# Turning h by transposing transfers in every tile of a state-space scan with a quantized gated FFN

## The reference

```
xc = conv(in_proj(ctx));  u = silu(xc + b)
dt = softplus(dt_proj(x_proj(u)[:16]) + b);  B, C = x_proj(u)[16:32], x_proj(u)[32:48]
state = state * exp(dt * A) + (dt * u) * B      # 16 states, over 512 positions
y = (sum over the states of state * C + D * u) * silu(layernorm(x))
x = x + tanh(g_x) * y

def bitlinear(x, w):                  # activations and weights fake-quantized
    xq = round(clip(rms(x) * s)) / s          # s = 127 / max|rms(x)|
    wq = round(clip(w / mean|w|, -1, 1)) * mean|w|
    return xq @ wq.T
n = layernorm(x)
h = silu(bitlinear(n, w_gate)) * bitlinear(n, w_up)      # 2048 wide
x = x + tanh(g_ffn) * bitlinear(h, w_down)
```

## Time and profile before

| | |
|---|---|
| median of 3 runs | 612.37 us (612.18 to 612.91) |
| the profiled execution | 611.89 us, of it 609.9 us span |
| busy: PE, PEld | 516.7 us (85%), 359.8 us (59%) |
| busy: DVE, ACT, POOL | 556.6 us (91%), 507.7 us (83%), 521.0 us (85%) |
| L889 POOL, b products | 117, 2364 ns each |
| L515 and L509 PE, transposes | 1024 and 528 |
| L615 PE, transposes of h | 176, 24.0 us in all |
| transfers of b, c | 1024.0 KB and 512.0 KB, median 6.7 and 6.5 us to landing |

### The profile page before, as it was taken

The page is one execution under the profiler, slowest core; times in us unless marked ns, Lnnn a source line. Parts: engine busy times, 40 slices in busy tenths (PEclk is TensorE's granted clock), DMA queues, the critical chain, the costliest instruction groups (busy, mean ns, idle before and its releaser), DMA issues. The chain is left out here.

```text
span 609.9 us, 9603 instructions
## 1 busy us (share of the span) xinstructions
PE 516.7 (85%) x3190; PEld 359.8 (59%) x3190; DVE 556.6 (91%) x766; ACT 507.7 (83%) x776; POOL 521.0 (85%) x298
## 2 busy tenths in 40 slices
PE   6999676768675888989879898989789999998997
PEld 2443265747564676767656767675667575764443
DVE  1899989999999899999899999998999999988774
ACT  3879788986999789899978898998798989777773
POOL 1558799999999899999999899999998999973340
PEclk9999859778799999999999999999999999999999
DMA  8992951530661010115521111145411110000323
GB/s 273 403 412 108 325 197 34 192 136 1 240 243 53 0 53 2 35 34 208 203 93 35 34 37 36 35 157 223 121 35 35 36 36 18 1 18 21 84 53 86
DMA packets 38866, 66.32 MB, mean 109 GB/s; under 512 B 12177, under 2 KB 20369, under 8 KB 36002
## 3 DMA queue, kind: packets, MB, share of 16 engines
q1 hardware_dynamic: 38818, 65.72, 30.9%
HBM read 55.49 MB, written 8.13 MB: 104 GB/s over the span
## 5 line engine op out<-in xcount | busy, mean ns | idle before, releaser
L889 POOL TENSOR_TENSOR area_s<-area_s,b_bc 128x1024 f32<-128x1024 f32 x117 | 275.2, 2364 | 14.1 <-DVE u_all L1510 9.9
L515 PE MATMUL pY<-ident,area_s 128*128 128x128 f32 x532 | 87.9, 291 | 54.5 <-DVE area_s L1518 54.5
L584 PE MATMUL pG<-wq_gu,area_f 128*128 128x512 fp8e4 x448 | 108.0, 380 | 4.2 <-ACT area_f L1106 2.9
L1510 DVE TENSOR_TENSOR_SCAN area_s<-pA,area_s 128x512 f32<-128x512 f32 x88 | 105.1, 1205 | 5.1 <-ACT pA L1169 5.1
L515 PEld LDWEIGHTS pY<-ident,area_s 128*128 128x128 f32 x532 | 62.2, 146 | 75.4 <-DVE area_s L1518 67.9
L1169 ACT ACTIVATE pA<-dt_all,a_neg 128x512 f32<-128x512 f32 x145 | 97.7, 682 | 10.7 <-DVE area_s L1510 5.9
L881 POOL TENSOR_TENSOR u_all<-u_all 128x1024 f32<-128x1024 f32 x44 | 103.9, 2361 | 0.2 <-DMA u_all<-bc_rows 0.2
L1518 DVE TENSOR_TENSOR area_s<-area_s,pC 128x512 f32<-128x512 f32 x132 | 87.0, 661 | 0.9 <-DVE area_s L1510 0.8
L509 PE MATMUL pC<-ident,xdT 128*128 128x128 f32 x528 | 84.2, 288 | 3.2 <-DVE area_s L1518 2.0
L584 PEld LDWEIGHTS pG<-wq_gu,area_f 128*128 128x128 bf16 x448 | 41.6, 98 | 48.9 <-ACT area_f L1106 5.2
L509 PEld LDWEIGHTS pC<-ident,xdT 128*128 128x128 f32 x528 | 65.4, 146 | 8.1 <-DVE area_s L1518 6.6
(11 more groups left out here) (218 smaller groups left out, 1123.0 us busy)
## 6 DMA issues: line engine op xcount, KB each, us to landing
b_bc<-bc_rows SPq DMA_DIRECT2D x14, 1024.0 KB, 6.7
area_s<-x SPq DMA_DIRECT2D x32, 256.0 KB, 2.9
u_all<-bc_rows SPq DMA_DIRECT2D x14, 512.0 KB, 6.5
b_bc<-w_gate SPq DMA_DIRECT2D x1, 4096.0 KB, 14.0
dt_all<-x SPq DMA_DIRECT2D x1, 4096.0 KB, 24.3
area_f<-w_up SPq DMA_DIRECT2D x1, 4096.0 KB, 33.6
area_f<-w_down SPq DMA_DIRECT2D x1, 4096.0 KB, 14.9
out<-area_f SPq DMA_DIRECT2D x16, 256.0 KB, 2.1
```

Source lines behind the costliest of these rows:

```text
L515: mm = pe.matmul(pY[:, k * P:(k + 1) * P], src[:, k * P:(k + 1) * P], ident[:, :], is_transpose=True, start=(first and k == 0), stop=(last ...
L584: mm = pe.matmul(bank, xqT[t % 2][:, k, :], wq_gu[:, k, m, c * GW:(c + 1) * GW], start=(k == 0), stop=(k == NT - 1))
L889: gp.tensor_tensor(db[c % NDB], du[s % 2].rearrange("p (a l) -> p a l", a=1).to_broadcast([P, CH, L]), b_bc[:, CH * c:CH * c + CH, :], ALU ...
L1510: dve.tensor_tensor_scan(h, at, dbu, 0.0, ALU.mult, ALU.add).then_inc(S["s_scan"], 1)
```

## The change

For tiles 0 to 10 TensorE's 16 transposes of h and ScalarE's four copies out of pG are gone. After scaling a half of h, ScalarE copies it, less MAGIC, as bf16 integers into the first half of the same place (`h_int`, function `whole_h`, semaphore f_ha), at n = 6 and 7. SP then issues a transposing transfer from there to `hqT` (`turn_whole`), the second half's when the first has landed. Since h of the next tile is written to the same place, `gate_silu` of chunk 0 waits for the first transfer and that of chunk 2 for the second. In the loading steps `turn_whole` stands behind three pieces of b and one of c; the fourth piece of b and the other three of c stand behind it. `down` of every tile waits for f_hqD. The tiles from 11 on are turned as before.

```diff
 
+        h_int = [carve(area_f, 1024 * i, F // 4, BF16) for i in range(2)]
         hb = [u_all[:, 2 + 2 * i:4 + 2 * i, :].rearrange("p n l -> p (n l)").bitcast(BF16) for i in range(2)]
...
 
-            def load_c(b):
+            def load_c(b, pairs=range(NP)):
                 for j, pair in enumerate(pooled(NT * b)):
+                    if j not in pairs:
+                        continue
                     if b and j < len(pooled(NT * b - 1)):
...
             load_u(3)
+            def turn_whole(t):
+
+                past(sp, S["f_dn"], t - 1)
+                for i in range(2):
+                    past(sp, S["f_hqD"], 32 * t + 16 * i)
+                    sp.wait_ge(S["f_ha"], 2 * t + i + 1)
+                    sp.dma_start_transpose(hqT[t % 2][:, i * FK // 2:(i + 1) * FK // 2, :], h_int[i]).then_inc(S["f_hqD"], 16)
+
             for s in range(NT, UNITS):
...
                 if s % NT == 0:
-                    load_b(s // NT)
-                    load_c(s // NT)
+                    load_b(s // NT, (0, 1, 2))
+                    load_c(s // NT, (0,))
+                if s >= 6:
+                    turn_whole(s - 6)
+                if s % NT == 0:
+                    load_b(s // NT, (3,))
+                    load_c(s // NT, (1, 2, 3))
                     load_c_alone(s // NT)
...
                 for i in range(2):
-                    past(sp, S["f_hqD"], 32 * (t - DMA_FROM) + 16 * i)
+                    past(sp, S["f_hqD"], 32 * t + 16 * i)
                     sp.wait_ge(S["f_hb"], 2 * (t - DMA_FROM) + i + 1)
...
 
+            turn_whole(DMA_FROM - 1)
             store(UNITS - 7)
...
                     pe.wait_ge(S["f_xqT"], t + 1)
-                    past(pe, S["f_hqT"], HR * t)
                 else:
...
 
-            def hq_transpose(t, r, banks):
-                pe.wait_ge(S["f_hm"], 2 * t + r // 2 + 1)
-                past(pe, S["f_hqT"], HR * t + r - 1)
-                for k in range(4):
-                    mm = pe.transpose(banks[r % 2][:, k * P:(k + 1) * P], h_of(t)[:, (4 * r + k) * P:(4 * r + k + 1) * P], ident[:, :])
-                mm.then_inc(S["f_hqp"], 1)
-
             def down(t, part, z_done):
                 if part == 0:
-                    if t < DMA_FROM:
-                        pe.wait_ge(S["f_hqT"], HR * t + HR)
-                    else:
-                        pe.wait_ge(S["f_hqD"], 32 * (t - DMA_FROM) + 16)
+                    pe.wait_ge(S["f_hqD"], 32 * t + 16)
                     past(pe, S["f_o"], t)
...
                 for k in range(part * DK, min(part * DK + DK, FK)):
-                    if k == FK // 2 and t >= DMA_FROM:
-                        pe.wait_ge(S["f_hqD"], 32 * (t - DMA_FROM) + 32)
+                    if k == FK // 2:
+                        pe.wait_ge(S["f_hqD"], 32 * t + 32)
                     mm = pe.matmul(pT[:, :], hqT[t % 2][:, k, :], wq_dn[:, k, :], start=(k == 0), stop=(k == FK - 1))
...
                 y_sum_pooled(s, 0)
-                if t2 >= 0:
-                    if t1 % NT:
-                        pe.wait_ge(S["f_xqT"], t1 + 1)
-                    hq_transpose(t2, 0, pG)
-                    hq_transpose(t2, 1, pG)
                 fill(s, 4, DPARTS)
-                if t2 >= 0:
-                    hq_transpose(t2, 2, pG)
-                    hq_transpose(t2, 3, pG)
                 y_sum(s, 6)
...
                     past(pe, S["f_h"], FC * t1)
-                    past(pe, S["f_hqT"], HR * t1 - 1)
                     xq_transpose(t1, pG[0])
...
                 act.wait_ge(S["f_gate"], FC * t + c + 1)
-                if t <= UNITS - NT:
-                    past(act, S["f_hqp"], HR * (t - (1 if t < UNITS - NT else 2)) + HR)
-                else:
+                if t < UNITS - NT and t and c % 2 == 0:
+                    act.wait_ge(S["f_hqD"], 32 * (t - 1) + (32 if c else 16))
+                elif t > UNITS - NT:
                     act.wait_ge(S["f_hb"], 2 * (t - 2 - DMA_FROM) + 2)
...
                 if t == UNITS - 1:
-                    act.wait_ge(S["f_hqD"], 32 * (t - 2 - DMA_FROM) + 32)
+                    act.wait_ge(S["f_hqD"], 32 * (t - 2) + 32)
                     junk = hb[t % 2]
...
 
-            def copy_hqT(t, r, banks):
-                act.wait_ge(S["f_hqp"], HR * t + r + 1)
-                past(act, S["f_dn"], t - 1)
-                act.activation(hqT[t % 2][:, 4 * r:4 * r + 4, :], banks[r % 2].rearrange("p (k t) -> p k t", t=P),
-                               ACT.Copy, bias=-MAGIC).then_inc(S["f_hqT"], 1)
+            def whole_h(t, i):
+
+                act.wait_ge(S["f_hm"], 2 * t + i + 1)
+                act.activation(h_int[i], h_main[:, i * F // 2:(i + 1) * F // 2], ACT.Copy, bias=-MAGIC).then_inc(S["f_ha"], 1)
 
...
                         copy_xqT(t1, pG[0][:, :])
+                    if n in (6, 7) and t2 >= 0:
+                        whole_h(t2, n - 6)
                     if n in (5, 6) and t2 >= 0:
...
                         x_variance(t1 + 1)
-                    if n in (7, 8) and t2 >= 0:
-                        copy_hqT(t2, 2 * n - 14, pG)
-                        copy_hqT(t2, 2 * n - 13, pG)
                     if s == PE_FROM - 1 and n in (2, 4, 6, 8):
...
```

More of the change, by code:

```diff
@@ L654, in down_quarter @@
             def down_quarter(t, r):
-                pe.wait_ge(S["f_hqT"], HR * DMA_FROM + r + 1)
+                pe.wait_ge(S["f_hqT"], r + 1)
                 for k in range(4 * r, 4 * r + 4):
@@ L803, in _ @@
                         end_transpose(1)
-                    pe.wait_ge(S["f_hqD"], 32 * (t - 1 - DMA_FROM) + (32 if k else 16))
+                    pe.wait_ge(S["f_hqD"], 32 * (t - 1) + (32 if k else 16))
                 mm = pe.matmul(down_bank(t - 1), hqT[(t - 1) % 2][:, k, :], wq_dn[:, k, :], start=(k == 0), stop=(k == FK - 1))
@@ L960, in h_whole @@
             def h_whole(t):
-                past(gp, S["f_hqD"], 32 * (t - DMA_FROM - 1))
+                past(gp, S["f_hqD"], 32 * (t - 1))
                 whole = [h_of(t)[:, i * F // 2:(i + 1) * F // 2] for i in range(2)]
@@ L967, in h_whole @@
                     if i == 0:
-                        gp.wait_ge(S["f_hm"], 2 * DMA_FROM + t - DMA_FROM + 1)
+                        gp.wait_ge(S["f_hm"], DMA_FROM + t + 1)
                     else:
@@ L1332, in _ @@
             for r in range(HR):
-                act.wait_ge(S["f_hqp"], HR * DMA_FROM + r + 1)
+                act.wait_ge(S["f_hqp"], r + 1)
                 act.activation(hqT[t % 2][:, 4 * r:4 * r + 4, :], end_bank(r).rearrange("p (k t) -> p k t", t=P),
```

2 lines of the change are left out of this document (1 added, 1 removed).

## The result

The changed kernel takes 625.51 us in the median of four runs (623.93 to 629.15), against 612.42 us of the kernel before on the same chip: a ratio of 1.0221, 95% interval 1.0175 to 1.0267. The prediction had the direction right (slower), but 625.51 lies outside its range of 611.8 to 620.5. The profiled execution took 624.89 us (span 623.1), 13.0 us more than that of before.

What follows compares the result with a forecast made beforehand. GpSimd and VectorE were taken as nearly full, VectorE the late one. The profiled 611.89 us plus 3.85 for queueing, other terms 0, gave 615.7; with 0.48 to the median, 616.2 us, range 611.8 to 620.5.

Steps and rivals of the forecast that it cites:

- ScalarE's and TensorE's part: Scan loop: ScalarE's swapped copies booked 0, up to 1.4 us for the range; TensorE's removed transposes booked 0.
- rival 2: Scan loop: `gate` 0 and 1 freed from pG and transposes, VectorE gains up to 3.7 us; 608.5 to 611 us; chance 0.09.
- The queueing term: Loading steps s = 7, s = 11: h's transfer moves behind the loads, delaying SiLU 1.75 and 2.37 us; sum 3.85; chance 0.61.
- my upper bound of 6.3: Loading steps: the whole 3.05 us landing follows the emptied queue, 3.0 + 3.6 - 0.27 = 6.3 us.
- the transfer's own data 1.37 us: Loading steps: time the data of h take once the loads are through, 1.03 + 0.34 = 1.37 us.
- Both delays meet a VectorE that is then waited for by GpSimd in the first steps of the next batch, so they stay: After s = 7 and s = 11: the loading steps' delays, 3.85 us in sum, are not recovered.
- Rival 3: s = 8, s = 12: thin TensorE work halves its clock, some 4 us a step, twice; 621 to 625 us; chance 0.08.
- The end at nothing: Last tiles, already turned by transfers: nothing moves but by the time the loop ends, 0 us.

Runs made afterwards that it cites:

- e1_order: Changed kernel with only the first quarter of b issued ahead of the transposing transfers in s = 7 and s = 11, other loads behind: 617.69 us.
- e7_again: The changed kernel run once more, with nothing altered: 628.13 us in one run.
- e2_busy: Changed kernel plus 16 unread transposes of the identity on TensorE in each step, in two groups of 8: 626.34 us.
- e6_src: Changed kernel with transposing transfers reading a fixed piece of the down weights, same size, and SiLU not waiting for them: 617.71 us.
- e5_place: Changed kernel with only the first quarter of b ahead, plus 16 identity transposes a step, placed where the removed ones stood: 612.55 us.
- e3_both: Changed kernel with only the first quarter of b ahead, plus 16 identity transposes a step, not waiting for ScalarE's scaling: 614.17 us.

## Why the prediction was wrong

- **Ordinary steps, ScalarE's and TensorE's part: right.** 30.35 us a step, no wait for a transfer, the copies no longer than those they replace. TensorE's relief gave nothing back (rival 2); in the one place where it showed, s = 11 of e1_order, it was 0.27 us, the very sum that I had booked.
- **The queueing term: right in mechanism, short in size.** The data of h do move behind the loads. I had a landing 6.9 us after the issue in s = 7; it took 7.8 to 9.5. The waits were 2.82 + 3.22 us against 1.75 + 2.37, within my upper bound of 6.3 in this profile, but 7.8 and 11.3 in e7_again and e2_busy. Two terms were too small. The loads of s = 7 were through not at 289.9 but shortly after 291: they went out 0.7 us later than before, and I had read the end of the third piece of b off the share of one window, 288.64, where the kernel before still moves data from 289 to 290 (share 0.04). And "the transfer's own data 1.37 us" were 1.6 us in s = 7, 2.8 in s = 11 (420.5 to 423.3) and up to 4.5 in e2_busy, because its packets stop and wait while the last ones of the loads are under way. My upper bound, a whole quiet landing behind the empty queue, was no bound.
- **The step that failed** is the sentence "Both delays meet a VectorE that is then waited for by GpSimd in the first steps of the next batch, so they stay": it stops there. I followed ScalarE's delay to VectorE and not to TensorE. `gate` 2 waits for the first SiLU, so a late SiLU empties TensorE, and the clock falls just when its work is due: 1.70 us at once in each loading step (1.43 net in s = 11), and some 0.3 behind the first. I had put this at nothing. e6_src shows the dependence: transfers as late, no wait, no fall.
- **Rival 3 happened, at a chance of 0.08.** I put it in s = 8 and s = 12, priced it at 4 us a step and weighed it low because of one thin stretch at 190 us that had kept its clock. It cost 1.74 and 2.15 us (e1_order), and about 1.6 and 0.4 in the changed kernel's profile. The idle stretch of some 4 us was read off the order correctly (4.26). I set it against queueing as if one excluded the other; they add (with the late transfers of the end they make the 625.5). The Trainium skill (page "TensorE: Matmul & The Clock Gate", section "Part 4: PE-mode transpose") says that transposes do not count as busy like matmuls. These runs speak against it: e5_place differs from e1_order in transposes alone and holds the clock in both of the steps in which e1_order loses it; e3_both, which also differs in them alone, holds it in s = 8.
- **The end at nothing: wrong by 1.46 us** in the profile. Nothing in its program changed. One transfer was late, and a packet of q8 lay in it; that the packet made it late is not shown.

With the order of the loads and transposes of the identity in place (e5_place), the change is worth nothing measurable (ratio 0.9998). It takes nothing from the two engines that bound the loop, so no version here beats the kernel before.

## What to carry to other kernels

Work taken from an engine that is not the bound was worth nothing here, and it cost the clock that this work had held up: before removing it, look at what else the engine does in that stretch, step by step, the odd steps too. Put a small transfer that somebody waits for ahead of the large loads, whichever queue carries them; how long one takes behind them is not the sum of its pieces. And follow a new wait to every engine that the waiting one feeds, not only to the bound.

## What was not expected of the hardware

- A transposing transfer of 128 x 1024 bf16 landed in 3.0 to 3.1 us in 81 of 96 cases at the quiet end of the kernel, in 3.0 to 4.1 us as the first behind 1 or 1.5 MB of loads (4.2 us for one second transfer, in e3_both, with a packet of q8 in it), and in 7.8 to 11.8 us behind 3 MB. On ScalarE's queue it took 6.7 and 8.6 us.
- Issuing such a transfer mostly held the issuing queue for 1.23 to 1.25 us, but SP's for 2.5 to 5.5 us when 3 MB of loads lay ahead.
- The 15 late transfers of the end, 3.9 to 4.8 us, each had a 16 KB packet of the queue "q8 instruction" begin 1.0 to 2.8 us after their issue; in the scan loop 15 others with one at 2.5 to 2.9 us landed in 3.0 to 3.3.
- With 12 or 16 fp32 transposes of 128 x 128 in each step, standing apart as before, the granted clock stayed at 1.00 in s = 8 and s = 12 of three profiles. Back to back they kept it in three stretches of four; four transposes, standing apart, in neither of two. What exactly decides it stays open.
